# A recommendation model on one core: each top-layer weight split once, the second top layer's halves read back from a DRAM scratch

## The reference

```
fm    = emb_table[arange(26), cat_idx]                # 2048 x 26 x 128, gathered rows
h     = relu(dense_x @ Wd1 + bd1)                     # 13 -> 512
h     = relu(h @ Wd2 + bd2)                           # 512 -> 256
dense = relu(h @ Wdf + bdf)                           # 256 -> 128
Z     = concat([fm, dense])                           # 27 features of 128
S     = einsum('bie,bje->bij', Z, Z)                  # all pairs
x     = concat([S[upper triangle], dense])            # 351 + 128 = 479
x     = relu(x @ Wt1 + bt1)                           # 479 -> 1024
x     = relu(x @ Wt2 + bt2)                           # 1024 -> 1024
x     = relu(x @ Wt3 + bt3)                           # 1024 -> 512
x     = relu(x @ Wt4 + bt4)                           # 512 -> 256
out   = sigmoid(x @ Wo + bo)                          # 256 -> 1
```

## Time and profile before

| what | value |
|---|---|
| median of 3 runs | 717.9 us |
| the profiled execution's own time | 719.22 us |
| its span | 717.4 us |
| PE busy | 612.2 us (85%) |
| POOL busy | 435.6 us (61%) |
| ACT busy | 399.6 us (56%) |
| DVE busy | 355.9 us (50%) |
| moved by DMA | 102.21 MB, mean 142 GB/s |
| granted TensorE clock, mean | 0.957 |

### The profile page before, as it was taken

One profiled execution on the slowest core, in us unless ns is written; L12 is line 12 of the kernel. 1 busy time (PEld: TensorE's weight loads), 2 busy tenths in 40 slices (PEclk: granted clock), 3 DMA queues, 4 the chain that ended last, 5 costly groups with the idle time before them and its releaser, 6 DMA issues.

```text
span 717.4 us, 19263 instructions
## 1 busy us (share of the span) xinstructions
PE 612.2 (85%) x8248; PEld 560.9 (78%) x8248; DVE 355.9 (50%) x579; ACT 399.6 (56%) x758; POOL 435.6 (61%) x421
## 2 busy tenths in 40 slices
PE   0776869899989988998999899897899888998997
PEld 0454558888888978897889778886899778997886
DVE  6441344555545645654463455453454454664553
ACT  2553545655665656664664566463564565666654
POOL 6777777667775777777757775577717776000000
PEclk9986878999999999999999999998899999999999
DMA  6444454767575657666666657565656657432552
GB/s 114 98 111 57 105 109 97 194 150 170 133 205 153 155 144 189 169 164 161 137 177 164 156 113 192 149 164 135 127 158 165 149 116 195 137 117 84 158 165 61
DMA packets 144104, 102.21 MB, mean 142 GB/s; under 512 B 12107, under 2 KB 137259, under 8 KB 143967
## 3 DMA queue, kind: packets, MB, share of 16 engines
q1 hardware_dynamic: 130274, 73.62, 34.6%
q0 software_dynamic: 13312, 27.29, 22.5%
q10 hardware_dynamic: 434, 0.08, 0.1%
HBM read 100.93 MB, written 0.01 MB: 141 GB/s over the span
## 4 chain that ended last, share of the span: by engine, by line
PE 48%; DMA 16%; DVE 14%; ACT 13%; issue 7%; SPq 2%; ACTq 0%
PE acc L499 35%; DMA raw<-w_t 15%; DVE strip L371 8%; PE unit L542 7%; ACT strip L423 7%; PE bank L529 5%; DVE feats L393 3%; ACT h L447 2%; ACT whole L446 2%; SPq L308 1%; PE acc L552 1%; DMA feats<-xT 1%; DVE rows L393 1%; DVE x L384 0%; DVE h L384 0%
## 5 line engine op out<-in xcount | busy, mean ns | idle before, releaser
L329 POOL DMA_INDIRECT gathered<-table,row_of x416 | 434.9, 1046 | 171.5 <-issue 124.6
L499 PE MATMUL acc<-h,strip 128*128 128x256 f32 (+1 forms) x2616 | 362.4, 296 | 36.8 <-ACT h L447 13.6
L499 PEld LDWEIGHTS acc<-h,strip 128*128 128x128 f32 x2616 | 335.6, 195 | 54.3 <-ACT h L447 22.6
L371 DVE TENSOR_TENSOR strip<-raw,strip 128x1024 fp32r<-128x1024 f32 (+2 forms) x152 | 174.7, 1150 | 145.2 <-ACT strip L423 141.0
L446 ACT ACTIVATE whole<-acc,bias 128x256 f32<-128x256 f32 (+1 forms) x184 | 92.3, 502 | 182.8 <-PE acc L499 179.3
L423 ACT ACTIVATE strip<-raw 128x1024 fp32r<-128x1024 f32 (+2 forms) x152 | 151.2, 996 | 43.9 <-DMA raw<-w_t 34.4
L384 DVE TENSOR_TENSOR h<-whole,h 128x256 fp32r<-128x256 f32 (+1 forms) x184 | 83.8, 459 | 176.0 <-ACT h L447 171.0
L499 PE MATMUL acc<-x,strip 128*128 128x256 f32 (+1 forms) x768 | 100.4, 293 | 2.8 <-DVE strip L371 2.8
L499 PEld LDWEIGHTS acc<-x,strip 128*128 128x128 f32 (+1 forms) x768 | 97.4, 200 | 4.7 <-issue 4.2
L447 ACT ACTIVATE h<-acc,bias 128x256 fp32r<-128x256 f32 (+1 forms) x184 | 91.8, 499 | 0.0
L542 PE MATMUL unit<-feats 128*27 128x26 f32 x4096 | 55.2, 195 | 22.3 <-issue 11.8
(11 more groups left out here) (33 smaller groups left out, 115.4 us busy)
## 6 DMA issues: line engine op xcount, KB each, us to landing
raw<-w_t SPq DMA_DIRECT2D x224, 256.0 KB
raw<-w_t SPq DMA_DIRECT2D x64, 128.0 KB
gathered<-table,row_of POOLq DMA_INDIRECT x416
raw<-w_t SPq DMA_DIRECT2D x32, 95.0 KB
raw<-w_d SPq DMA_DIRECT2D x8, 256.0 KB
raw<-w_df SPq DMA_DIRECT2D x8, 64.0 KB
feats<-xT SPq DMA_DIRECT2D x4, 104.0 KB
cat<-idx SPq DMA_DIRECT2D x1, 208.0 KB, 2.6
```

The lines of the kernel that those rows point to most:

```text
L329: nc.gpsimd.indirect_dma_start(gathered[:, t % SLOTS, c, :], None, table, bass.IndirectOffsetOnAxis(row_of[:, t, c:c + 1], 0)).then_inc(ga ...
L371: nc.vector.tensor_tensor(strip[:, slot, 1, 0:blocks, :], raw[:, slot, 0:blocks, :], strip[:, slot, 0, 0:blocks, :].bitcast(F32), ALU.subtract
L499: mm = nc.tensor.matmul(acc[:, slot, 0:width], strip[0:height, number % 2, a, k * together + m % together, :], given[0:height, b, k, :], s ...
```

## The change

The weights of t1, t3 and t4 are split once, during the start, and both halves stay in SBUF (`wt1`, `wt3`, `wt4`). Those of d2 and df are split once too. The t2 weights are split once, in a region `wt2` of three slots of 1 MB (both halves), each written by SP to a DRAM scratch `split_t2`; afterwards SP reads ready halves back, 1 MB for a strip. A part with an odd number walks the t2 strips from the last to the first, so the three strips in the slots serve twice; `t2_plan` finds 8 loads for the first part and 5 for each other. A load waits until the strip that last used its slot is done (`acc_done`).

The splitting has steps of its own ("piece", 19 of them: 1 d2, 1 df, 4 t1, 4 t3, 1 t4, 8 t2), each of 512 KB but df's of 128 KB: 2 before the first bottom, 3 after it, 3 after the second, 3 after the third, and all 8 of t2 after the fourth, ahead of the second tile's features. ACT and DVE meet them in their walk; PE skips them. `raw` keeps its two slots.

`whole` is gone: ACT writes the high half first and then the relu back into the accumulator in PSUM, DVE subtracts from PSUM, and PE waits for DVE too (`low_y`) before it uses the slot again. x shares memory with h2; FEATURES_AT is one strip earlier; the output leaves in 8 DMAs of ACT's queue, one per part.

```diff
-TOGETHER = {"d2": 2, "df": 1, "t1": 2, "t2": 1, "t3": 1, "t4": 1}
+PIECE = {"d2": (256, 1), "df": (128, 1), "t1": (256, 4), "t3": (128, 4), "t4": (256, 1), "t2": (128, 8)}
+PIECES = [(layer, m) for layer, (_, n) in PIECE.items() for m in range(n)]
+T2_SLOTS = 3
...
+    back = layer == "t2" and part[0] // CHUNK % 2
+    return reversed(range(n)) if back else range(n)
...
-FEATURES_AT = ((3, 4, 5, 6), (10, 11, 12, 13))
+FEATURES_AT = ((2, 3, 4, 5), (9, 10, 11, 12))
...
-STEPS = (bottom(0) + bottom(1) + features(PARTS[0], 0) + bottom(2) + bottom(3) + features(PARTS[0], 1)
-         + regroups(PARTS[0]) + stacks(PARTS[0]) + strips_of(PARTS[0], "t1"))
+STEPS = (pieces(*PIECES[0:2]) + bottom(0) + pieces(*PIECES[2:5]) + bottom(1) + pieces(*PIECES[5:8])
+         + bottom(2) + pieces(*PIECES[8:11]) + features(PARTS[0], 0) + bottom(3) + pieces(*PIECES[11:])
+         + features(PARTS[0], 1) + regroups(PARTS[0]) + stacks(PARTS[0]) + strips_of(PARTS[0], "t1"))
...
+def t2_plan():
+    held, used, slot_of, loads = [None] * T2_SLOTS, [-1] * T2_SLOTS, {}, []
+    for n in ACC_STEPS:
+        if STEPS[n][0] == "strip" and STEPS[n][2] == "t2":
+            m = STEPS[n][3]
+            if m not in held:
+                k = min(range(T2_SLOTS), key=lambda j: used[j])
+                held[k] = m
+                loads.append((m, k, used[k]))
+            k = held.index(m)
+            used[k] = SO_FAR[n]["acc"]
+            slot_of[n] = (k, sum(1 for one in loads if one[1] == k))
+    return slot_of, loads
...
SP:
+            for number, (layer, m) in enumerate(PIECES):
                 if number >= 2:
                     sp.wait_ge(low_w, number - 1)
...
+                    sp.dma_start(to, w[layer][:, cols].rearrange("(k p) n -> p k n", p=P)).then_inc(raw_in[slot], 16)
+                if number > T2_FIRST:
+                    k = number - 1 - T2_FIRST
+                    sp.wait_ge(low_w, number)
+                    sp.dma_start(split_t2[k], t2_bits[:, k % T2_SLOTS]
+                                 ).then_inc(t2_out[k % T2_SLOTS], 16)
...
+            for m, k, used in T2_LOADS:
+                if used >= 0:
+                    sp.wait_ge(acc_done, used + 1)
+                sp.dma_start(t2_bits[:, k], split_t2[m]).then_inc(t2_in[k], 16)
...
DVE:
-                    given = (acc if kind == "stack" else whole)[0:height, now["acc"] % ACCS, 0:step[1][1]]
+                    given = acc[0:height, now["acc"] % ACCS, 0:step[1][1]]
                     nc.vector.tensor_tensor(parts[1], given, parts[0].bitcast(F32), ALU.subtract).then_inc(low_y, 1)
-                if strips_ahead(at) and SO_FAR[at + 1]["strip"] + 1 < len(STRIPS):
-                    split_strip(SO_FAR[at + 1]["strip"] + 1)
+                if kind == "piece":
+                    number = now["piece"]
+                    dve.wait_ge(high_w, number + 1)
+                    nc.vector.tensor_tensor(piece_target(number, 1), piece_raw(number),
+                                            piece_target(number, 0).bitcast(F32), ALU.subtract).then_inc(low_w, 1)
...
ACT:
-                        nc.scalar.activation(whole[0:height, slot, 0:width], source, func, bias=b)
-                        nc.scalar.activation(parts[0], source, func, bias=b).then_inc(acc_read, 1)
+                        nc.scalar.activation(parts[0], source, func, bias=b)
+                        nc.scalar.activation(source, source, func, bias=b).then_inc(acc_read, 1)
...
+                if kind == "piece":
+                    number = now["piece"]
+                    if number == T2_FIRST:
+                        act.wait_ge(acc_done, SO_FAR[at]["acc"])
+                    if number >= T2_FIRST + T2_SLOTS:
+                        k = number - T2_FIRST
+                        act.wait_ge(t2_out[k % T2_SLOTS], 16 * (k // T2_SLOTS))
+                    act.wait_ge(raw_in[number % 2], raw_landed(number))
+                    nc.scalar.activation(piece_target(number, 0), piece_raw(number), ACT.Copy).then_inc(high_w, 1)
...
PE:
                     pe.wait_ge(acc_read, before + 1)
-                    if STEPS[ACC_STEPS[before]][0] == "stack":
+                    if COUNTS[ACC_STEPS[before]]["split"]:
                         pe.wait_ge(low_y, splits_by(before))
...
+                    if layer == "t2":
+                        k, loads = T2_SLOT[at]
+                        pe.wait_ge(t2_in[k], 16 * loads)
+                        strip = t2_slots[k]
+                    else:
+                        n = PIECE[layer][0]
+                        pe.wait_ge(low_w, PIECES.index((layer, m * P // n)) + 1)
+                        strip = weights[layer][:, :, :, m * P:(m + 1) * P]
```

More of the change, by code:

```diff
@@ L50, with t2_order, pieces @@
 BIASES = 29
-TOGETHER = {"d2": 2, "df": 1, "t1": 2, "t2": 1, "t3": 1, "t4": 1}
+PIECE = {"d2": (256, 1), "df": (128, 1), "t1": (256, 4), "t3": (128, 4), "t4": (256, 1), "t2": (128, 8)}
+PIECES = [(layer, m) for layer, (_, n) in PIECE.items() for m in range(n)]
+T2_SLOTS = 3
 def strips_of(part, *layers):
-    return [("again" if m % TOGETHER[layer] else "strip", part, layer, m)
-            for layer in layers for m in range(LAYERS[layer][3])]
+    return [("strip", part, layer, m) for layer in layers for m in t2_order(part, layer)]
+def t2_order(part, layer):
+    n = LAYERS[layer][3]
+    back = layer == "t2" and part[0] // CHUNK % 2
+    return reversed(range(n)) if back else range(n)
+def pieces(*which):
+    return [("piece", None, layer, m) for layer, m in which]
 def bottom(q):
@@ L104 @@
 HALVES = {"flip": (range(0, 4), range(4, len(FLIPS))), "regroup": (range(0, 4), range(4, len(REGROUPS)))}
-KINDS = ("acc", "split", "strip", "bank", "unit", "tile", "dense")
+KINDS = ("acc", "split", "piece", "bank", "unit", "tile", "dense")
 def counts(step):
     kind = step[0]
-    split = kind in ("spread", "stack") or (kind in ("strip", "again") and step[2] not in ("df", "t4"))
-    return {"acc": int(kind in ("spread", "strip", "again", "stack", "out")), "split": int(split),
-            "strip": int(kind == "strip"),
+    split = kind in ("spread", "stack") or (kind == "strip" and step[2] not in ("df", "t4"))
+    return {"acc": int(kind in ("spread", "strip", "stack", "out")), "split": int(split),
+            "piece": int(kind == "piece"),
             "bank": len(HALVES[kind][step[-1]]) if kind in HALVES else 0,
@@ L144, in made_at @@
             made = ("x", s[2])
-        elif s[0] in ("strip", "again"):
+        elif s[0] == "strip":
             made = (LAYERS[s[2]][1], s[3])
@@ L153, in upto, with piece_dmas, raw_landed @@
     return (number + (not odd)) // 2
[L156 to L164, removed]
+def piece_dmas(number):
+    return 3 if PIECES[number][0] == "t1" else 1
+def raw_landed(number):
+    return 16 * sum(piece_dmas(n) for n in range(number % 2, number + 1, 2))
+T2_FIRST = PIECES.index(("t2", 0))
 def dlrm(nc, xT, idx, table, ident, w1, w, biases, wo, bo, out):
@@ L185, in dlrm @@
         h4 = sb("h4", [P, 2, CHUNK])
-        whole = sb("whole", [P, 2, WIDE])
         dense = sb("dense", [P, B])
-        raw = sb("raw", [P, 2, 8, P])
-        strip = sb("strip", [P, 2, 2, 8, P], F32R)
+        raw = sb("raw", [P, 2, 1024])
+        wt1 = sb("wt1", [P, 2, 4, 1024], F32R)
+        wt3 = sb("wt3", [P, 2, 8, 512], F32R)
+        wt4 = sb("wt4", [P, 2, 4, 256], F32R)
+        wt2 = sb("wt2", [P, T2_SLOTS, 2, 1024], F32R)
         eye = sb("eye", [P, P])
@@ L266, in dense_made @@
             n = max(n for n, s in enumerate(STEPS)
-                    if s[0] in ("strip", "again") and s[2] == "df" and s[1][0] <= part[0])
+                    if s[0] == "strip" and s[2] == "df" and s[1][0] <= part[0])
             return SO_FAR[n + 1]["acc"]
@@ L415, in _ @@
             act.wait_ge(constants_in, 16 * 4)
[L417 to L427, removed]
+            nc.scalar.activation(y[0:1, 0, 0:1], bo_s[0:1, 0:1], ACT.Sigmoid)
             for at, step in enumerate(STEPS):
@@ L432, in _ @@
                     act.wait_ge(acc_done, number + 1)
-                if kind in ("spread", "strip", "again", "stack"):
+                if kind in ("spread", "strip", "stack"):
                     height, parts, plain, column = acc_target(step)
@@ L505, in _ @@
                 if kind == "out":
-                    h4_at = max(n for n in range(at) if STEPS[n][0] in ("strip", "again") and STEPS[n][2] == "t4")
+                    h4_at = max(n for n in range(at) if STEPS[n][0] == "strip" and STEPS[n][2] == "t4")
                     pe.wait_ge(acc_read, SO_FAR[h4_at + 1]["acc"])
```

96 lines of the change are left out of this document (54 added, 42 removed).

## The result

The changed kernel took 742.7 us (median of 4 runs, 740.6 to 743.9) against 718.4 for the kernel before on the same chip: ratio 1.033, 95% interval 1.027 to 1.040, slower. The forecast was slower, 762 us, with a range of 732 to 792. The sign, the cause and the place were right; of the +44 that were forecast, +24 came. An execution that took over 1.5% longer than the fastest of its kernel counts as slow, and the ratios here leave slow ones out.

What follows compares the result with a forecast made beforehand. The prediction took PE to bound the periods and a chain to bound the start. Start 178.2, periods 522.0 and tail 61.1 gave a written span of 762.3, adjusted to about 762 us, range 732 to 792.

Steps and rivals of the forecast that it cites:

- The start: Stretch up to the first t1: added piece loads, t2 pieces and held slot lengthen it from 111.7 to 178.2 us.
- groups: Start, three pieces after a bottom: the third waits for the first's raw slot, 8.0 us each, 24.0 for three.
- t2 block: Start, eight t2 pieces with nothing beside them, loads behind 1 MB stores: about 41 us, +39.
- The periods: Seven stretches from one t1 to the next: 544.9 falls by 22.9 to 522.0 us, 74.6 a period.
- what the splits cost PE: Periods: PE's waits on ACT, weight halves, banks and tiles shrink, -21.8 us.
- Issue gaps and clock: Periods: 12.7 us of issue gaps and about 11 from the low clock; 9 of the 24 taken as gained.
- odd parts: Ahead of t3, which needs h2 block 0, now made last: 1.45 us, three times in the periods, 4.4.
- the held slot: Accumulator slot held until DVE is done: +3.5 us in the periods, +3.5 in the start, +0.5 in the tail.
- The cheap start: Rival: third loads cost transfer only, stores ride beside loads, periods fall to 71 us: 707 us, chance 0.05.
- The cold start: Rival: in the start, all that follows a PE stop runs at the low clock level: 781 us, chance 0.13.
- The loads did not bind at 1 MB a strip: Rival: t2 loads bind; at 6.2 us for 1 MB about 845 us, at 5 us about 785; chance 0.10.
- Periods did not stay at 77.8: Rival: the waits don't go, gaps move to issue, clock and held slots, periods stay at 77.8: 785 us, chance 0.08.

Runs made afterwards that it cites:

- e1: Changed kernel with the pieces of t1, t3 and t4 singly in the bottoms instead of in groups of three: 730.4 us, ratio 1.011 to the kernel before.
- e4: Changed kernel with 64 KB instead of 1 MB in each t2 store and read-back: 718.5 us, ratio 0.996 to the kernel before.
- b1: Kernel before, with ACT and DVE splitting only the first 128 of 1024 values of a strip's row, all loads kept: 664.2 us, ratio 0.925.
- e6: Changed kernel with the relu kept in SBUF again (whole), accumulator slot free once ACT has read it: 732.1 us, ratio 1.023 to the kernel before.
- e3: Changed kernel with t1, t3, t4 pieces singly in the bottoms and t2's spread to the end of the first t1: 715.7 us, ratio 0.989.
- e7: Changed kernel with each 1 MB read-back preceded by another of the same 1 MB into raw: 862.2 us, ratio 1.197 to the kernel before.
- c2: Changed kernel with all pieces spread, t2's slightly earlier, whole back in SBUF, t3 backwards in odd parts: 689.5 us, ratio 0.960 to the kernel before.
- b2: Kernel before with only DVE's half of the weight split cut to 128 of 1024 values, ACT splitting whole strips: 685.3 us against 720.8.
- c3: Changed kernel with each 1 MB read-back as four DMAs of 256 KB, rows of 2 KB: 744.5 us, ratio 1.034 to the kernel before.

## Why the prediction was right, and where it was off

**The start** (forecast +66.5, measured +65.2). Right in its places: groups 24 against 22, t2 block 39 against 35, the rest 3.5 against 8. That the total is right to 1.3 us is partly luck: these errors cancel, and starts of the same code spread by 6 us. The rest of 8 is not explained. e1 shows that the groups' cost is their place in ACT's order, e4 that the stores are nearly a third of the block (36 to 25 us). Mis-sized in it: 1 MB with 8 KB rows. I took 3.5 us of engine time and 6.3 to land. This row gives the landing of the eight stores of wt to split_t (the view has none for the read-backs), 5.2 in the middle:

```profile
DMA to landing us min/median/max: 3.9/5.2/10.7
```

The Trainium skill (DMA: Bandwidth & Descriptors, Bandwidth) has 6.15 us for 1 MB in its table, measured for DMAs that GpSimd issues; SP issued these, and the trace has 5.2. The estimate of the block from that page, some 5 us cheaper than mine, was the better one (34 against the 35 measured).

**The periods** (forecast -22.9, measured -37.4) hold the error, and it is the term of what the splits cost PE. I took 21.8 us out of PE's wait rows, and 9 of issue and clock, 30.8 in all. b1 measures the whole at 45.8. I went wrong twice. The waits with a named releaser in those rows come to 26.6 us, and I kept 4.8 of them; all went, with 1.9 us of smaller ones. And beyond the clock I took PE's busy time as fixed, when some 10 us of it were matmuls held up and counted as busy. Issue gaps and clock were taken about right: the gaps went from 12.7 to 11.1 us and the mean clock from 0.98 to 0.99, which is some 6 us. Of the added terms odd parts were right, 4.4 (4.4 measured), and the held slot too small, 3.5 (6.4 in e6's profile). The check by parts: 499.1 (b1, no splits) + 4.4 + 6.4 = 509.9 against 507.5. But it leaves no room for e4's 8 us of read-backs, unless b1's own loads (73.62 MB) cost as much: that was not tried.

**The sum.** 178.2 + 522.0 + 61.1 is 761.3, not the 762.3 that the prediction wrote; with 1.8 around it and 1.3 off it is still about 762.

**The tail** (forecast +0.3, measured -3.2): the same term; b1's tail is 53.8 against 60.8.

**The read-backs** (forecast 0): no wait, as forecast; e4 shows a price of 8 us by another way, which none of my steps had.

**The rivals.** The cheap start (707) did not happen, though e3, by order alone, has its first t1 at 124, well before that rival's 149.9; its total is 715.7, as the periods did not fall to 71. The cold start was partly there: the clock in the start fell from 0.80 to 0.67, and PE's busy time there rose by 4 us only, so it cost little. The Trainium skill (TensorE: Matmul & The Clock Gate, Part 1) has the clock at half rate after idling; the trace agrees, but standing still costs far more than the slow matmuls behind it: PE is idle 89 us of the start (161.3 - 72.3) where it was 28 (96.1 - 67.9). The loads did not bind at 1 MB a strip and did at 2 (e7). Periods did not stay at 77.8.

## What to carry to other kernels

Work that is taken out of a loop has to be paid somewhere: ask in which engine's in-order list it lands, and who is behind it there. The splitting of nineteen pieces lengthened the start by 65 us as blocks and by 12 when it was spread (c2, which also has whole back), with a stop of 8.7 us behind it. And to price work that lies beside the bound engine, cut its size in the kernel as it is: the 21.8 us that I took from the wait rows were half of what the cut showed, in part because the profile counts a held-up matmul as busy.

## What the runs showed of the hardware

**Gathers and DVE.** A gather's instruction on POOL took 1046 ns in the mean before, and without DVE's strip subtraction, with ACT's as before (b2), 962:

```profile
L329 POOL DMA_INDIRECT gathered<-table,row_of x416 | 400.0, 962 | 179.9 <-issue 124.7 <-DVE feats L401 52.0 <-DVE prods L342 3.2
```

In the changed kernel it is 958, and 980 with whole back in SBUF (e6). So it is DVE's subtraction with both inputs in SBUF that lengthens gathers. The Trainium skill (SBUF — State Buffer, Who interferes with whom) says that such an instruction contends with GpSimd ones that read SBUF; the trace agrees. Here POOL was no bound, so it bought nothing.

**Row size.** From 190 to 215 us the changed kernel's queue, reading 8 KB rows, moved 4.94 MB in 55.2% of 25 us, 358 GB/s, against 297 with mostly 512-byte rows. Other things differ between the two as well, and rows of 2 KB (c3) left the time as it was:

```profile
q1 hardware_dynamic: 667, 4.94, 55.2%
```
